# Attention phase of a fused kernel: heads in pairs, a tile in four steps, three rotating banks

## What is computed

```python
h = shift_token(x)
q, k, v = split(h @ wqkv)                 # 8 heads of 64
q, k = rotary_xpos(l2norm(q) * qs, l2norm(k) * ksc)
sim = where(mask, -max, q*8 @ k.T)        # window of 256, look back 256
o = softmax(sim) @ v
x = x + o @ wo
```

## Time and profile before

| | before |
|---|---|
| median of 3 runs | 3989.9 us (3986.2 to 3994.1) |
| the profiled execution | 3991.4 us, its span 3989.6 us |
| busy time of TensorE, VectorE, ScalarE, GpSimd | 3761.0, 2227.7, 1561.7, 1187.1 us |
| share of the span | 94%, 56%, 39%, 30% |
| granted clock of TensorE, mean of the span | 0.972 of full speed |

### The profile page before, as it was taken

How to read it: one execution, slowest core, us unless ns; L and a number is a source line. 1 busy time by engine, 2 the same in 40 slices (tenths; PEclk the granted TensorE clock), 3 DMA queues, 4 the chain that set the end, 5 groups by cost and what they waited for, 6 DMA issues and landing times. The chain is left out here.

```text
span 3989.6 us, 57450 instructions
## 1 busy us (share of the span) xinstructions
PE 3761.0 (94%) x21008; PEld 2966.7 (74%) x21008; DVE 2227.7 (56%) x5258; ACT 1561.7 (39%) x3973; POOL 1187.1 (30%) x1044
## 2 busy tenths in 40 slices
PE   5899895999999997999999969999999979999998
PEld 4666664777777775888888857777777768887887
DVE  5777764777777775323322247777777753222331
ACT  4655653555554553211111135455555531111211
POOL 2333432444444441111111134444444301111111
PEclk8999997999999998999999979999999989999999
DMA  4112113111111113211111121111111141111112
GB/s 123 38 38 71 54 59 128 46 47 55 57 56 47 50 47 106 102 58 59 58 59 58 48 100 56 53 49 56 57 56 46 43 134 62 58 59 58 58 58 74
DMA packets 220780, 253.74 MB, mean 64 GB/s; under 512 B 33337, under 2 KB 147778, under 8 KB 220501
## 3 DMA queue, kind: packets, MB, share of 16 engines
q1 hardware_dynamic: 220501, 250.07, 19.2%
HBM read 142.62 MB, written 90.61 MB: 58 GB/s over the span
## 5 line engine op out<-in xcount | busy, mean ns | idle before, releaser
L1700 DVE SCALAR_TENSOR_TENSOR u_full<-banks,b_cols,gate 128x512 f32<-128x512 f32 (+1 forms) x176 | 132.1, 750 | 890.5 <-ACT gate L1642 793.7
L45 PE MATMUL banks<-fxT_h,w_h 128*128 128x512 f32 (+1 forms) x1408 | 558.8, 397 | 4.8 <-DVE fxT_l L1692 4.8
L47 PE MATMUL banks<-fxT_h,w_l 128*128 128x512 f32 (+1 forms) x1408 | 558.1, 396 | 0.0
L46 PE MATMUL banks<-fxT_l,w_h 128*128 128x512 f32 (+1 forms) x1408 | 556.6, 395 | 0.0
L1642 ACT ACTIVATE gate<-banks,b_cols 128x512 f32<-128x512 f32 (+1 forms) x176 | 121.2, 689 | 1029.0 <-PE banks L47 1029.0
L998 POOL TENSOR_TENSOR rn<-ssq,neg_half 128x8 f32<-128x8 f32 x128 | 211.3, 1651 | 825.4 <-DVE ssq L1304 825.0
L1231 ACT ACTIVATE pT_h<-banks 128x384 fp32r<-128x384 f32 x512 | 251.4, 491 | 426.0 <-PE banks L1101 424.1
L1224 ACT ACTIVATE prob<-neg_s,neg_m 128x384 f32<-128x384 f32 x512 | 314.2, 614 | 83.7 <-DVE neg_m L1337 83.4
L45 PE MATMUL banks<-pT_h,v_h 128*64 128x128 f32 x1536 | 339.3, 250 | 1.0 <-DVE pT_l L1291 0.8
L45 PE MATMUL banks<-wqkv_h,hT_h 128*128 128x512 f32 x768 | 316.3, 412 | 18.2 <-DVE wqkv_l L1287 9.3
L45 PEld LDWEIGHTS banks<-fxT_h,w_h 128*128 128x128 f32 (+1 forms) x1408 | 260.8, 185 | 75.1 <-DVE fxT_l L1692 10.8
(11 more groups left out here) (174 smaller groups left out, 8765.8 us busy)
## 6 DMA issues: line engine op xcount, KB each, us to landing
y_in<-y_rows SPq DMA_DIRECT2D x64, 256.0 KB, 2.9
z_rows<-y_in SPq DMA_DIRECT2D x64, 256.0 KB, 2.0
f_res<-z_rows SPq DMA_DIRECT2D x16, 1024.0 KB, 5.5
f_x<-x_rows SPq DMA_DIRECT2D x16, 1024.0 KB, 8.0
y_rows<-f_res SPq DMA_DIRECT2D x16, 1024.0 KB, 4.3
out_rows<-f_x SPq DMA_DIRECT2D x16, 1024.0 KB, 4.8
w_ffn_stage<-in_w SPq DMA_DIRECT2D x30, 512.0 KB, 4.7
x_in<-in_x SPq DMA_DIRECT2D x10, 1024.0 KB, 6.7
```

The source lines that it names most:

```text
L45: pe.matmul(out, a_h, b_h, start=start, stop=False)
L46: pe.matmul(out, a_h, b_l, start=False, stop=False)
L47: return pe.matmul(out, a_l, b_h, start=False, stop=stop)
L1700: e.scalar_tensor_tensor(out=u_full[r, m % 2, :], in0=ps[r, 2 * (m % 2), :], scalar=b1[r, m, 0:1], in1=gate[r, :], op0=ALU.add, op1=ALU.mu ...
```

## The change

Nothing changes in what is computed. In `attention_phase`, on TensorE, ScalarE and VectorE:

- `scores(t, p)` issues the six matmuls of heads 2p and 2p+1 in turn, one on rows 0 to 63 and one on rows 64 to 127, into banks 2 and 3. It waits until both scores of the pair before are out of these banks.
- A tile t is four steps p. On TensorE a step is: scores of the next pair, `transpose_p` of this pair, one dense product, `values` of this pair. The dense product is v of tile t+1 (step 0), `transpose_h` of t+2 and `output` of t-1 (step 1), `transpose_qk` of t+1 and q of t+2 (step 2), k of t+2 (step 3).
- All outputs stand in bank 6 (O_BANK); banks 0, 1 and 7 go round for the seven dense products and transposes of a tile (`turn`). So each of these waits until the third before it is out of its bank.
- VectorE's `divide` takes one reciprocal for two heads, and its order is by steps too, as is ScalarE's.

SyncE's and GpSimd's programs stay as they are. The diff, cut to its core:

```diff
+        O_BANK = 6
+
+        def turn(n):
+            return (0, 1, 7)[n % 3]
+
+        def bank_qkv(t, a):
+            return turn(7 * t if a == 2 else 7 * t - 2 + a)
+
+        def bank_h(t):
+            return turn(7 * t - 6)
+
+        def bank_y(t):
+            return turn(7 * t + 16)
+
+        def bank_r(t, a):
+            return turn(7 * t + 3 + a)
...
-    e.wait_ge(s["dv_s"], at(LH, i, 4 * HEADS, n - 1))
-    r = slice(DH * (h % 2), DH * (h % 2) + DH)
-    uu = u % 4
-    split_matmul(e, ps[:, 2 + h % 2, 0:KEYS], [x[r, uu % 2, h // 2, :] for x in qT],
...
+    e.wait_ge(s["dv_s"], nth(LH, HEADS * t + 2 * p))
+    for a, b in ((0, 0), (0, 1), (1, 0)):
+        for odd in range(2):
+            r = slice(DH * odd, DH * odd + DH)
+            last = e.matmul(ps[:, 2 + odd, 0:KEYS], qT[a][r, t % 2, p, :],
+                            kT[b][r, p, t % 4:t % 4 + 3, :].rearrange("p a k -> p (a k)"),
+                            start=a + b == 0, stop=a == 1)
+            if a == 1:
+                last.then_inc(s["pe_s"], 1)
...
+def project(t, a):
+    e.wait_ge(s["dv_h"], nth(NT, t + 1))
+    if a == 0:
+        e.wait_ge(s["dv_y"], nth(NT, t - 2))
+    else:
+        e.wait_ge(s["dv_r"], nth(2 * NT, 2 * t - 1 if a == 1 else 2 * t))
...
+def output(t):
+    e.wait_ge(s["dv_o"], nth(2 * NT, 2 * t + 2))
+    e.wait_ge(s["dv_norm"], nth(2 * NT, min(2 * t + 6, 2 * NT)))
...
+for t in range(NT):                       # TensorE
+    for p in range(4):
+        if p < 3:
+            scores(t, p + 1)
+        else:
+            scores(t + 1, 0)
+        transpose_p(t, 2 * p)
+        transpose_p(t, 2 * p + 1)
+        if p == 0:
+            project(t + 1, 2)
+        elif p == 1:
+            transpose_h(t + 2)
+            output(t - 1)
+        elif p == 2:
+            transpose_qk(t + 1)
+            project(t + 2, 0)
+        else:
+            project(t + 2, 1)
+        values(t, 2 * p)
+        values(t, 2 * p + 1)
...
+for t in range(NT):                       # VectorE
+    for p in range(4):
+        if p == 0:
+            lo_o(t - 1, 1)
+        elif p == 2:
+            lo_o(t, 0)
+        for h in (2 * p + 2, 2 * p + 3):
+            masked(t + h // HEADS, h % HEADS)
+        if p == 0:
+            norms(t + 1, 1)
+        elif p == 1:
+            lo_v(t + 1)
+        elif p == 2:
+            residual(t - 1)
+        else:
+            norms(t + 2, 0)
+        lo_p(t, 2 * p)
+        lo_p(t, 2 * p + 1)
+        if p == 1:
+            normalise(t + 1, 1)
+            lo_h(t + 2)
+        elif p == 2:
+            lo_qk(t + 1)
+        if p < 3:
+            divide(t, p + 1)
+        else:
+            divide(t + 1, 0)
+            normalise(t + 2, 0)
```

More of the change, by code:

```diff
@@ L1041, in transpose_h @@
                     for k in range(DC):
-                        last = e.transpose(ps[:, 0, k * P:(k + 1) * P], h_in[:, j % 4, k * P:(k + 1) * P], ident[:])
+                        last = e.transpose(ps[:, bank_h(t), k * P:(k + 1) * P], h_in[:, t % 4, k * P:(k + 1) * P], ident[:])
                     last.then_inc(s["pe_h"], 1)
-                def project(i, j, a):
-                    if not tile_exists(i, j):
+                def project(t, a):
+                    if t >= NT:
                         return
+                    e.wait_ge(s["dv_h"], nth(NT, t + 1))
@@ L1117, in values @@
                     last.then_inc(s["pe_o"], 1)
-                def output(i, u):
-                    if u < 0 and i == 0:
+                def output(t):
+                    if t < 0:
                         return
-                    if u == 0 and i == 0:
+                    if t == 0:
                         e.wait_ge(w_lo, w.done(w.count))
[L1125 to L1130, removed]
+                    e.wait_ge(s["dv_o"], nth(2 * NT, 2 * t + 2))
+                    e.wait_ge(s["dv_norm"], nth(2 * NT, min(2 * t + 6, 2 * NT)))
@@ L1169, in _ @@
[L1169 to L1172, removed]
+                    project(0, a)
+                transpose_h(1)
+                transpose_qk(0)
+                project(1, 0)
+                project(1, 1)
+                e.wait_ge(s["pl_init"], 4 * l + 4)
+                scores(0, 0)
+                for t in range(NT):
[18 more added lines that the diff above has]
+                        values(t, 2 * p + 1)
@@ L1174, in _ @@
+                output(NT - 1)
             @block.scalar
@@ new lines, in lo_qk @@
+                def lo_qk(t):
+                    if t < NT:
+                        for a in range(2):
+                            e.wait_ge(s["ac_r"], nth(2 * NT, 2 * t + a + 1))
+                            hi, out = ((qT[x][:, t % 2] if a == 0 else kT[x][:, :, 2 + t % 4, :]) for x in range(2))
+                            e.tensor_tensor(out, ps[:, bank_r(t, a), :].rearrange("p (c t) -> p c t", c=DC), hi.bitcast(F32),
+                                            ALU.subtract).then_inc(s["dv_r"], 1)
@@ L1371, in _ @@
-                lo_h(0, 0)
+                    e.wait_ge(s["pe_w"], nth(NT, t + 1))
+                    e.wait_ge(s["ld_y"][t % 4], 16 * (l * NI + t // 4 + 1))
+                    e.tensor_tensor(y_in[:, t % 4, :], ps[:, bank_y(t), :], y_in[:, t % 4, :], ALU.add).then_inc(s["dv_y"], 1)
+                lo_h(0)
                 rest_of_weights(0, 2 * DC)
-                norms(0, 0, 0)
+                norms(0, 0)
                 rest_of_weights(2 * DC, 3 * DC)
-                normalise(0, 0, 0)
@@ L1376, in _ @@
-                norms(0, 0, 1)
+                normalise(0, 0)
+                norms(0, 1)
                 rest_of_weights(3 * DC, w.count)
-                normalise(0, 0, 1)
+                normalise(0, 1)
                 e.wait_ge(s["ld_small"], 16 * 10 * l + 16 * 9)
                 e.wait_ge(s["pl_init"], 4 * l + 4)
-                lo_v(0, 0)
-                lo_qk(0, 0)
-                lo_h(0, 1)
-                masked(0, 0, 0)
-                masked(0, 0, 1)
-                divide(0, 0, 0)
@@ L1420, in _ @@
-                for i in range(NI):
-                    body(i)
-                lo_o(NI - 1, 3, 1)
-                residual(NI - 1, 3)
+                lo_v(0)
+                lo_h(1)
+                lo_qk(0)
+                norms(1, 0)
+                normalise(1, 0)
+                masked(0, 0)
+                masked(0, 1)
+                divide(0, 0)
+                for t in range(NT):
+                    for p in range(4):
+                        if p == 0:
+                            lo_o(t - 1, 1)
+                        elif p == 2:
+                            lo_o(t, 0)
+                        for h in (2 * p + 2, 2 * p + 3):
+                            masked(t + h // HEADS, h % HEADS)
+                        if p == 0:
+                            norms(t + 1, 1)
+                        elif p == 1:
+                            lo_v(t + 1)
+                        elif p == 2:
+                            residual(t - 1)
[3 more added lines that the diff above has]
+                        lo_p(t, 2 * p + 1)
+                        if p == 1:
+                            normalise(t + 1, 1)
+                            lo_h(t + 2)
+                        elif p == 2:
+                            lo_qk(t + 1)
[4 more added lines that the diff above has]
+                            normalise(t + 2, 0)
@@ L1426, in ffn_sems @@
+                lo_o(NT - 1, 1)
+                residual(NT - 1)
 def ffn_sems(sem):
```

361 lines of the change are left out of this document (137 added, 224 removed).

## The result

| | before | after |
|---|---|---|
| median | 3992.0 us (4 runs, 3986.2 to 3995.9) | 4043.8 us (4 runs, 4039.5 to 4044.9) |
| ratio, 95% interval | | 1.0129 (1.0111 to 1.0146) |
| profiled execution, its span | 3991.4, 3989.6 us | 4044.9, 4043.1 us |
| mean granted clock | 0.972 | 0.957 |

The account below looks back on a forecast made before the run. TensorE bounds the kernel; pairs and fewer shape changes save 3.5 us a tile, waits return 3.4, the clock adds 0.94: 27.3 against 26.46. Over 58 tiles +49, layer ends +4: 4043 us, range 3960 to 4090.

Parts of the forecast that it names:

- The pairs: Attention scores on TensorE: two heads side by side cost about one head, saving 3.2 us a tile with fewer shape changes.
- rival D: Interleaved scores of two heads do not run side by side: 1.5 us more a tile, 4075 us; chance 0.05.
- The ends of V: Entering and leaving the value matmuls, now behind dense work: 0 to 0.36 us a tile, taken as 0.
- steps 0 and 3: The first and last of a tile's four TensorE steps: no such bank wait, 5.40 us each.
- Step 1: Output of tile t-1 waits for VectorE's normalise of k: TensorE stands 2.3 us (2.1 as counted), step takes 8.1.
- Step 2: q's projection of tile t+2 waits for VectorE's residual: TensorE stands 1.2 us (1.0 as counted), step takes 7.5.
- rival A: Waits come as walked but TensorE's clock holds: 26.4 us a tile, 3988 us, up to 4009; chance 0.18.
- The waits: TensorE's dense products wait for VectorE to empty one of three banks, late at two places: 3.4 us a tile.
- Rival B: The bank waits do not form and TensorE stays the bound: 22.9 us a tile, 3787 us; chance 0.17, partial included.
- The clock: The 2.1 us TensorE gap brings half clock: 0 to 1.7 us a tile, 0.94 taken, making the tile 27.3.
- rival C: The half clock hits every attention tile: 28.1 us a tile, 4087 us; chance 0.10.
- The ends of a layer: One more product before the first scores, no first wait in the first tile: +2 us a layer, +4 in all.

Follow-up runs that it names:

- e6: Changed kernel with VectorE's normalise and residual moved first in their steps, but the two heads' scores issued apart, transposes between: 3982.9 us, ratio 0.9983 to kernel before.
- e3: Changed kernel with VectorE's normalise at the head of step 1 and residual at the head of step 2: 3763.0 us, ratio 0.9431 to the kernel before.
- e5: Changed kernel plus 16 unused transposes of the identity on TensorE ahead of output, filling the idle gap: 3991.7 us, ratio 1.0002 to the kernel before.
- e2: Changed kernel with only VectorE's residual moved to the head of step 2, ahead of lo_o: 3971.6 us, ratio 0.9951 to the kernel before.
- e4: Changed kernel with VectorE's normalise of k moved between the two lo_p of step 1: 3965.2 us, ratio 0.9939 to the kernel before.
- e1: Changed kernel with only VectorE's normalise moved to the head of step 1, ahead of the two masked: 3842.5 us, ratio 0.9633 to the kernel before.
- e7: Changed kernel with normalise and residual both first in their steps, each pair's six score matmuls issued head by head: 3766.3 us, ratio 0.9437 to kernel before.

## Why the prediction came out

**The pairs.** Rows of x2, 0.45 apart, as forecast; rival D falls. I had 3.2 us a tile for them; e6 shows 3.5.

**The ends of V.** From 0 to 0.36 a tile was left open, and 0 was taken. The last dense matmul and the first value matmul are 0.22 apart (1104.37 to 1104.59), no more than two dense ones, and 0.15 lead from the values to the scores: 0 was right.

**The steps.** 5.40 was forecast for steps 0 and 3, 5.35 and 5.37 were measured. Step 1: 8.1 and 8.12. Step 2: 7.5 and 7.56. The 0.3 us by which the walk undercounted a tile before did not come back: 26.4 was forecast at the full clock, and 26.45 measured.

**The sums.** Redone, two of them come out a little otherwise. One step is 0.73 + 0.63 + 2.8 + 1.22 = 5.38 and not 5.40, and rival A's sum gives 3990 us and not 3988. More telling is the balance of 3.5 us saved and 3.4 given back. By e3, which has no waits, the saving is 26.46 - 22.76 = 3.70 us, and the waits take 26.45 - 22.76 = 3.69. Both were put too low, by about as much, since a step with a wait is as long as VectorE's chain, whatever TensorE needs before it.

**The waits.** Idle 2.1 and 1.0 were forecast, 2.10 and 1.11 measured, and what ends them is what was named. Adding up VectorE's instructions ahead of the awaited one from the start of the scores gave the step to 0.06 us. Rival B (no waits, 3787) falls, and e3 shows what it would have been worth. It gives 3763, better than that sum: the tile is 22.76 and not 22.9 (8 us in 58 tiles), and the ends, for which I had added 4, gain some 15 (the spans differ by 230.1, of which 58 x 3.70 = 214.6 is steady state). Some 7 us of that a layer are the earlier first `output` in the tile that I didn't count; there, too, scores come in pairs.

**The clock.** Apart from the ends of V this was the one term without a row of its own kind, and it made the whole of the forecast slowdown but the 4 us of the ends. I took 0.94 us a tile, a little over half of 1.7; it is 0.84, from 1.58 in 53% of the tiles. Rival A (the clock holds) is e5's time, 3992, and rival C (every tile) would have been 4087. The share was a guess between two rows that disagreed. Taken as a chance it came near; in fact the tiles with and without a stretch follow a pattern, for which there was no row to read, and e2 shows how much the share moves: 68% for a gap of the same length. With that share the changed kernel would have come to 58 x 0.15 x 1.58 = 14 us more. The nearness of 4043 to 4044 is partly luck. The mean clock over 900 to 1500 us is the 0.97 that was forecast.

The place is as forecast, within 2 us of the gap; in this tile it begins at once. TensorE by time behind the wait in the slower tile, changed kernel; 0.43 from start to start is already the half clock (0.23 at the full one):

```profile
1141.69 0.56 PE L45 MATMUL banks<-wo_h,oT_h 128*128 128x512 f32 x1 [2.11 <-DVE qk L1300]
1142.05 0.63 PE L46 MATMUL banks<-wo_l,oT_h 128*128 128x512 f32 x1
1142.48 0.63 PE L47 MATMUL banks<-wo_h,oT_l 128*128 128x512 f32 x1
```

**The ends of a layer.** +4 was forecast. Of the 53.5 us by which the spans differ, 58 x 0.83 = 48.1 are steady state by layer 0's tile, which leaves 5.4.

## What to carry over

When work on the bounding engine is regrouped into larger steps, walk the other engines' order once from the moment each step hands over, and put first whatever the bounding engine will wait for, if its inputs are already there: two such instructions moved the kernel from 1.3% slower to 5.7% faster. A regular idle gap on TensorE has to be priced at its own length and again at the half clock it may bring, and a gap that is a little shorter can be free of the second. A mean over tiles can hide that there are two kinds: look at several neighbours one by one. Busy time alone would have passed this change: 152 us less of it, and 52 us more in all.

## What was not expected of the hardware

- A gap of 2.1 us between transposes and dense matmuls, once a tile, brings a stretch at half clock (1.2 GHz, 1.58 us of loss) in 15 of 28 tiles, in a kernel whose tiles are otherwise alike, and in 19 of 28 where the tile without a stretch is 1.4 us shorter (e2). A gap of 1.6 us brings none (e4), nor does one of 1.1 (e1), nor the gap of 2.1 when 1.9 us of it are filled with transposes (e5). Which tiles are hit follows a pattern: every second one in the changed kernel but for two places in a layer, mostly two of three in e2. What sets the pattern, and where between 1.6 and 2.1 us the gap begins to matter, no run here shows. The Trainium skill, "TensorE: Matmul & The Clock Gate", section "A second HAM failure mode: psum-queue depth-cycling", tells of a kernel that cycles through PSUM banks and whose clock goes to and fro with short idles between groups of matmuls; the tiles of 26.45 and 28.03 us here agree with that. The banks alone don't bring it here, since e3 cycles through the same ones without the idle gaps, at a clock of 1.00.
- Matmuls on the two halves of the rows run side by side even when three of one half are issued before three of the other (e7, 3766 against 3763 us).
- The way into matmuls on half of the rows costs 0.09 us from dense work and 0.16 from transposes (e6). The way from dense work to matmuls on half of the columns costs nothing that the rows show (0.22 from start to start).
